# Running the experts of 24 of 32 token tiles on gathered rows, in a transformer layer on one core

## The reference, cut to what matters

```python
x1 = _layer_norm(x + attn_out, ln1_w, ln1_b)
gates = jax.nn.softmax(x1 @ gate_w.T + gate_b, axis=-1)
_, top_idx = jax.lax.top_k(gates, TOP_K)          # TOP_K = 2 of NE = 8
top_gates = jnp.take_along_axis(gates, top_idx, axis=-1)
expert_outputs = jnp.einsum('bsd,efd->bsef', x1, expert_w) + expert_b[None, None]
sel = jnp.take_along_axis(expert_outputs, top_idx[..., None], axis=2)
moe_out = jnp.sum(sel * top_gates[..., None], axis=2)
return _layer_norm(x1 + moe_out, ln2_w, ln2_b)
```

## Time and profile before

| | |
|---|---|
| median of three runs | 1448.19 us (1446.72 to 1450.09) |
| the profiled execution's own time | 1447.28 us |
| its span | 1445.5 us |
| TensorE busy | 1384.9 us, 96% |
| VectorE busy | 1089.6 us, 75% |
| ScalarE busy | 783.6 us, 54% |
| GpSimd busy | 428.0 us, 30% |
| mean granted TensorE clock | 0.993 |

### The profile page before, as it was taken

The page is one execution under the profiler, slowest core; times in us unless marked ns, Lnnn a source line. Parts: engine busy times, 40 slices in busy tenths (PEclk is TensorE's granted clock), DMA queues, the critical chain, the costliest instruction groups (busy, mean ns, idle before and its releaser), DMA issues.

```text
span 1445.5 us, 28119 instructions
## 1 busy us (share of the span) xinstructions
PE 1384.9 (96%) x9600; PEld 773.2 (53%) x9600; DVE 1089.6 (75%) x2736; ACT 783.6 (54%) x1707; POOL 428.0 (30%) x707
## 2 busy tenths in 40 slices
PE   7899999999999999999999999999999999999995
PEld 6767655554455445354656655555443355555542
DVE  3765877887787887778655897888778787888745
ACT  3235365555665555666655445554656467665651
POOL 4434522322232231122343543333121110111233
PEclk9999999999999999999999999999999999999997
DMA  3865422230211121120116232222120011111100
GB/s 116 201 172 128 124 57 61 58 85 21 63 46 46 38 62 33 40 57 20 50 49 156 79 90 68 57 57 65 29 60 21 22 24 29 33 32 33 34 23 12
DMA packets 152560, 88.57 MB, mean 61 GB/s; under 512 B 114430, under 2 KB 145974, under 8 KB 152163
## 3 DMA queue, kind: packets, MB, share of 16 engines
q1 hardware_dynamic: 152419, 86.78, 23.2%
HBM read 60.71 MB, written 25.43 MB: 60 GB/s over the span
## 4 chain that ended last, share of the span: by engine, by line
PE 44%; DVE 4%; ACT 3%; issue 2%; SPq 2%; DMA 2%; POOL 1%; POOLq 0%; DVEq 0%; ACTq 0%
PE bank L1537 11%; PE bank L1424 10%; PE bank L1401 8%; PE bank L1373 7%; ACT pbuf L978 2%; DVE mxs L1065 2%; SPq L806 1%; DMA qs<-nmT 1%; PE bank L1494 1%; PE bank L1377 1%; PE bank L1406 1%; PE bank L1513 1%; PE bank L1472 1%; PE bank L1480 1%; PE bank L1523 1%
## 5 line engine op out<-in xcount | busy, mean ns | idle before, releaser
L1065 DVE TENSOR_REDUCE mxs<-bank 128x1 f32<-128x512 f32 (+3 forms) x1120 | 709.4, 667 | 150.1 <-PE bank L1373 79.6
L978 ACT ACTIVATE pbuf<-bank 128x512 f32<-128x512 f32 (+1 forms) x1112 | 588.6, 599 | 326.1 <-PE bank L1401 151.0
L1401 PE MATMUL bank<-qs,ks 99*128 99x256 bf16 (+3 forms) x1536 | 420.7, 319 | 16.4 <-DMA qs<-nmT 10.9
L1373 PE MATMUL bank<-ks,qs 96*128 96x512 bf16 (+3 forms) x1280 | 423.0, 349 | 4.9 <-DVE mxs L1065 2.5
L1424 PE MATMUL bank<-pbuf,vcur 128*17 128x256 f32 (+3 forms) x3072 | 253.5, 469 | 0.3
L1401 PEld LDWEIGHTS bank<-qs,ks 99*128 99x128 bf16 x1536 | 142.3, 98 | 172.1 <-issue 56.3
L1537 PE MATMUL bank<-ew,x1T 128*128 128x512 f32 x464 | 222.4, 601 | 0.4 <-DVE mxs L1065 0.3
L1373 PEld LDWEIGHTS bank<-ks,qs 96*128 96x128 bf16 x1280 | 123.3, 98 | 129.7 <-issue 40.6
L1424 PEld LDWEIGHTS bank<-pbuf,vcur 128*17 128x17 f32 x3072 | 79.8, 97 | 147.4 <-issue 109.6
L1537 PEld LDWEIGHTS bank<-ew,x1T 128*128 128x128 f32 x464 | 82.0, 190 | 72.3 <-issue 60.8
L958 ACT ACTIVATE etmp<-bank,small 128x256 f32<-128x256 f32 x116 | 48.7, 471 | 80.1 <-PE bank L1537 80.1
(11 more groups left out here) (279 smaller groups left out, 1746.2 us busy)
## 6 DMA issues: line engine op xcount, KB each, us to landing
vcur<-v_scratch SPq DMA_DIRECT2D x92, 136.0 KB, 2.3
parts_scratch<-parts SPq DMA_DIRECT2D x29, 384.0 KB, 3.3
xw<-windows SPq DMA_DIRECT2D x29, 256.0 KB, 2.8
qs<-parts_scratch SPq DMA_DIRECT2D x32, 192.0 KB, 3.3
ks<-parts_scratch SPq DMA_DIRECT2D x28, 192.0 KB, 3.4
qs<-parts_scratch SPq DMA_DIRECT2D x32, 128.0 KB, 3.1
v_scratch<-vst SPq DMA_DIRECT2D x29, 136.0 KB, 2.4
x_scratch<-x SPq DMA_DIRECT2D x29, 128.0 KB, 1.7
```

Of the source, the lines that this page charges most:

```text
L978: nc.scalar.activation(pbuf[:, u0:u0 + heads, nj * P - cols:nj * P], bk[:, 0:heads * cols].rearrange("p (h t) -> p h t", h=heads), ACT.Exp)\
L1065: v.reduce_max(mxs[:, j * HJ + h:j * HJ + h + heads, c], bk[:, 0:heads * cols].rearrange("p (h t) -> p h t", h=heads), AX_X)\
L1373: last = mm(bk[:, x * cols:(x + 1) * cols].rearrange("p (n t) -> p n t", t=P), qs5[0:KR, pos % QRING, j, head, :], ks5[0:KR, kslot, 0:cols ...
L1401: last = mm(bk[:, x * cols:(x + 1) * cols].rearrange("p (n t) -> p n t", t=P), ks5[0:KR + NPART, kslot, kb % GT, head, :], qs5[0:KR + NPAR ...
```

## The change

The first 24 tiles (`SPARSE`) of the order of the `d_` and `f_` steps take another way through the experts; the last 8 stay dense. They are handled in 3 chunks of 8 tiles (`CHUNK`):

- For each tile, five small VectorE steps (`f_A`, `f_A12`, `f_as`, `f_Rb`, `f_gt`) and one on TensorE (`f_rk`, two small bf16 multiplications) count how many rows of the chunk went to the same expert before each row. `f_acc0` adds x1 and the expert bias into `rD`. `f_st` stores x1 and this sum to DRAM; the next tile's `d_res` waits for the one store and its `d_aff` for the other.
- After 8 tiles, `t_cnt` and `t_tab` (15 small VectorE instructions) work out for each of a row's two choices its place in a list of 23 blocks of 128 rows (`BLOCKS`), each block with one expert only. `t_sc` is 16 indirect transfers from GpSimd that scatter each row's number and its weight to these places in DRAM; `t_id` loads the list back in pieces of 8 bytes.
- For each of the 23 blocks: SP reads the block's expert from a register and loads its matrix, 256 KB (`s_w`), GpSimd gathers 128 rows of x1 (`s_g`), TensorE transposes them (`s_T`) and multiplies them with the one expert (`s_e`, four 128x256 instructions), ScalarE copies twice (`s_Tc`, `s_ec`, the second with the weight as scale), SP stores the block (`s_st`).
- For each tile again: `b_load` brings back the sum of `f_acc0`, `b_g1` and `b_g2` are indirect transfers from GpSimd that gather the row's two results and add them in; the `h_` steps are the `g_` steps in buffers of their own, without `g_y`.
- All this has 16 KB of its own in each partition (`gathering`). `pbuf` gives them up: `VRUN` goes from 4 to 2, so a `pv` run covers 2 key tiles and there are 192 runs in place of 100.
- `plan()` has the new steps, with 1300 ns for each indirect transfer on GpSimd and 2200 ns until it has landed (`INDIRECT`).

The core of the diff:

```diff
-VRUN = 4
+VRUN = 2
...
+INDIRECT = {"s_g": 2200, "b_g1": 2200, "b_g2": 2200, "t_sc": 2200}
...
+SPARSE = 24
+CHUNK = 8
+CHUNKS = SPARSE // CHUNK
+BLOCKS = 2 * CHUNK + NE - 1
...
+            add("f_A", T, "DVE", 100, ("f_ixf", T), ("t_tab", c - 1), ("w_tri8", 0))
+            add("f_A12", T, "DVE", 90, ("f_A", T), ("f_rk", T - 1), ("f_as", T - 1))
+            add("f_rk", T, "PE", 200, ("f_A12", T), ("f_as", T - 1), ("w_lists", 0))
+            add("f_as", T, "DVE", 90, ("f_rk", T), ("t_cnt", c - 1))
+            add("f_Rb", T, "DVE", 90, ("f_rk", T), ("t_tab", c - 1))
+            add("f_gt", T, "DVE", 90, ("f_top", T), ("t_sc", c - 1))
+            add("f_st", T, "SP", 900, ("f_acc0", T))
...
+                add("t_sc", c, "POOL", 2 * CHUNK * 1300, ("t_tab", c), ("load_dummy", 0))
+                add("t_id", c, "SP", 2500, ("t_sc", c), ("s_st", c * BLOCKS - 1))
...
+                    add("s_w", u + x, "SP", 900, ("t_tab", c), ("s_e", u + x - 2), ("w_o", 0))
+                    add("s_g", u + x, "POOL", 1300, ("t_id", c), ("f_st", last), ("s_T", u + x - 2))
+                    add("s_T", u + x, "PE", 215, ("s_g", u + x), ("s_e", u + x - 1))
+                    add("s_Tc", u + x, "ACT", 300, ("s_T", u + x), ("s_e", u + x - 2))
+                    add("s_e", u + x, "PE", 900, ("s_Tc", u + x), ("s_w", u + x))
+                    add("s_ec", u + x, "ACT", 300, ("s_e", u + x), ("s_st", u + x - 2))
+                    add("s_st", u + x, "SP", 900, ("s_ec", u + x))
...
+        gathering = sb("gathering", [P, 4096])
...
+                elif name == "t_sc":
+                    pool.wait_ge(tab_step, TABS * (T + 1))
+                    pool.wait_ge(dummy_stored, 16 * CHUNKS)
+                    for x in range(2 * CHUNK):
+                        pool.indirect_dma_start(id_dram[T], bass.IndirectOffsetOnAxis(ap=placed[:, x:x + 1], axis=0),
+                                                own[:, x // 2, x % 2, :], None).then_inc(ids_stored, 16)
...
+                    pool.indirect_dma_start(accB, None, ys_dram[T // CHUNK], bass.IndirectOffsetOnAxis(
+                        ap=placed[:, 2 * (T % CHUNK) + k:2 * (T % CHUNK) + k + 1], axis=0), compute_op=ALU.add)\
+                        .then_inc(gathered, 16)
```

More of the change, by code:

```diff
@@ L307, in stage_steps @@
-        add("f_e0", T, "PE", 1720, ("d_x1Tc", T))
+        if T < SPARSE:
+            c, u = T // CHUNK, T // CHUNK * BLOCKS
+            add("f_acc0", T, "DVE", 330, ("f_b", T), ("d_aff", T))
+            add("f_A", T, "DVE", 100, ("f_ixf", T), ("t_tab", c - 1), ("w_tri8", 0))
[5 more added lines that the diff above has]
+            add("f_st", T, "SP", 900, ("f_acc0", T))
+            i = T % CHUNK
+            last = c * CHUNK + CHUNK - 1
+            add("b_load", T, "SP", 450, ("f_st", T), ("h_aff2", T - 1))
+            add("b_g1", T, "POOL", 1300, ("t_tab", c), ("s_st", u + BLOCKS - 1), ("b_load", T))
+            add("b_g2", T, "POOL", 1300, ("b_g1", T))
+            back = c * CHUNK + CHUNK - 1 + 6 + 1.2 + (2.6 + 0.5 * i if c < CHUNKS - 1 else 1.3 + 0.25 * i)
+            rows["b_load", T] = *rows["b_load", T][:2], back - 0.3, rows["b_load", T][3]
+            rows["b_g1", T] = *rows["b_g1", T][:2], back - 0.2, rows["b_g1", T][3]
+            rows["b_g2", T] = *rows["b_g2", T][:2], back - 0.1, rows["b_g2", T][3]
+            if i == CHUNK - 1:
+                add("t_cnt", c, "PE", 150, ("f_as", T))
+                add("t_tab", c, "DVE", 3500, ("t_cnt", c), ("f_Rb", T), ("f_gt", T), ("b_g2", c * CHUNK - 1), ("s_st", c * BLOCKS - 1), ("w_tri8", 0))
+                add("t_sc", c, "POOL", 2 * CHUNK * 1300, ("t_tab", c), ("load_dummy", 0))
+                add("t_id", c, "SP", 2500, ("t_sc", c), ("s_st", c * BLOCKS - 1))
+                base = last + 6 + 1.2
+                for name in ("t_cnt", "t_tab", "t_sc", "t_id"):
+                    rows[name, c] = *rows[name, c][:2], base, rows[name, c][3]
+                for x in range(BLOCKS):
+                    add("s_w", u + x, "SP", 900, ("t_tab", c), ("s_e", u + x - 2), ("w_o", 0))
[5 more added lines that the diff above has]
+                    add("s_st", u + x, "SP", 900, ("s_ec", u + x))
+                    for k, name in enumerate(("s_w", "s_g", "s_T", "s_Tc", "s_e", "s_ec", "s_st")):
+                        rows[name, u + x] = *rows[name, u + x][:2], base + 0.1 + (2.5 if c < CHUNKS - 1 else 1.2) * x / BLOCKS + k / 100, rows[name, u + x][3]
+            add("h_load", T, "SP", 450, ("b_g2", T), ("st0", tile), ("h_store", T - 1))
+            add("h_st", T, "DVE", 330, ("b_g2", T))
+            add("h_mv", T, "DVE", 100, ("h_st", T))
+            add("h_rstd2", T, "POOL", 950, ("h_mv", T))
+            add("h_xb", T, "POOL", 700, ("h_load", T), ("h_rstd2", T))
+            add("h_norm2", T, "DVE", 370, ("h_mv", T))
+            add("h_aff2", T, "DVE", 370, ("h_norm2", T), ("h_xb", T))
+            add("h_zst", T, "DVE", 330, ("h_aff2", T))
+            add("h_zmv", T, "DVE", 100, ("h_zst", T))
+            add("h_rstd3", T, "POOL", 950, ("h_zmv", T))
+            add("h_norm3", T, "DVE", 320, ("h_rstd3", T))
+            add("h_store", T, "SP", 450, ("h_norm3", T))
+            for k, name in enumerate(("load", "st", "mv", "rstd2", "xb", "norm2", "aff2", "zst", "zmv", "rstd3", "norm3", "store")):
+                rows["h_" + name, T] = *rows["h_" + name, T][:2], back + k / 32, rows["h_" + name, T][3]
+            continue
@@ L1291, in _ @@
                 elif name in ("f_e0c", "f_e2c"):
                     k = int(name[3])
-                    half = e0_half if k == 0 else e2_half
                     dve.wait_ge(*fill(name[:4], T))
@@ L1532, in _ @@
                     mm(bk[:, 0:E], wT[f], ebp[:, :], start=True, stop=True).then_inc(filled[b], 1)
+                elif name == "f_rk":
+                    pe.wait_ge(hot12_ready, T + 1)
+                    pe.wait_ge(lists_ready, LISTS)
+                    last = mm(bk[:, 0:NE], tri, hot12, start=True, stop=T % CHUNK == 0)
+                    if T % CHUNK:
+                        pe.wait_ge(hotsum_ready, T)
+                        last = mm(bk[:, 0:NE], one, hotsum, start=False, stop=True)
+                    last.then_inc(filled[b], 1)
+                elif name == "t_cnt":
+                    pe.wait_ge(hotsum_ready, (T + 1) * CHUNK)
+                    mm(bk[:, 0:NE], one, hotsum, start=True, stop=True).then_inc(filled[b], 1)
+                elif name == "s_T":
+                    pe.wait_ge(xslot_loaded[T % 2], 16 * (T // 2 + 1))
+                    for c in range(EC):
+                        last = tr(bk[:, c * P:(c + 1) * P], xslot[T % 2][:, c * P:(c + 1) * P], idf[:, :])
+                    last.then_inc(filled[b], 1)
+                elif name == "s_e":
+                    pe.wait_ge(*drain("s_T", T))
+                    pe.wait_ge(wslot_loaded[T % 2], 16 * (T // 2 + 1))
+                    for c in range(EC):
+                        last = mm(bk[:, 0:E], xTslot[T % 2][:, c, :], wslot[T % 2][:, c, :], start=c == 0, stop=c == EC - 1)
+                    last.then_inc(filled[b], 1)
                 elif name in ("f_e0", "f_e1", "f_e2", "f_e3"):
```

397 lines of the change are left out of this document (335 added, 62 removed).

## The result

The changed kernel takes 1471.06 us (median of 5 executions, 1464.71 to 1473.57) against 1448.19; the ratio is 1.0147, with a 95% interval of 1.0123 to 1.017. The forecast was 1395 us, with 1362 to 1441 for 8 in 10. So it is slower, by about 23 us, and outside the range. The profiled execution took 1464.71 us, the fastest of the five, of which 1462.6 are the span shown here.

A forecast was written before the change was run, and what follows sets the result against it. TensorE's work was taken to bound the kernel: -78.9 us there brings the profiled 1447.3 to 1368.4, plus 16 for VectorE and 10 for late transfers gives 1394.4, with 0.9 for the median 1395 us; 8 in 10 from 1362 to 1441.

The forecast's parts named there:

- VectorE's pace: From 166 to 600 us VectorE, at 87%, would make the stretch 16 us longer than TensorE alone; bounds 0 and 51.
- late transfers and GpSimd's bursts: Late normalisations behind 16 indirect transfers in one piece and late gathers at the blocks' `s_T`: 10 us, bounds 0 and 138.
- The added work: On TensorE: 69 blocks 75.2 us, ranking 2.9 us, 92 more `pv` runs 12.9 us.
- ScalarE's longer wait for `pv`: Short `pbuf` rival: `ex` waits 92 times more, 110 us, mostly covered; if two fifths reach TensorE, 1439 us; chance 15%.
- The run length: `VRUN` from 4 to 2: 92 more `pv` runs at 0.14 us each on TensorE, 12.9 us.
- What another engine takes back: VectorE's added steps against TensorE's need, by stretch: 16 us from 166 to 600 us, nothing in the later stretches.
- Transfers and queues: About 50 MB more transfers, 216 more SP issues, 165 indirect transfers at 1.3 us on GpSimd: 10 us in all.
- SP's queue: Sign of failure: one queue, SP's above all, holds `nm_st` back for several us in each job.
- The serial path of a tile: The next tile's `d_res` waits for this tile's stored sum: 20 to 30 us, covered by a tile's 39 us, costed at nothing.

The follow-up runs named there:

- The half steps: The kernel before with half of the expert matmuls of its first 24 tiles left out: 1394.20 us in the old order, 1385.99 us when planned for.
- the kernel with neither: The changed kernel with the 48 adding gathers and the 48 scatters left out, order kept: 1432.04 us, ratio 0.9885.

## Why the prediction was wrong

The sum was -78.9 us for TensorE, +16 for VectorE's pace, +10 for late transfers and GpSimd's bursts, -53 in all. Measured is +22.9, so 76 us are missing. By its own steps:

**The added work was sized well.** The blocks cost 69 us against 75.2. The issue of a plain gather or a scatter took 0.97 to 0.99 us against 1.3, that of an adding gather 1.63. ScalarE's longer wait for `pv` came and was mostly covered. The run length cost 18.4 us against 12.9.

**"What another engine takes back": the removed work was not worth its time.** This is the first step that failed. It asked only whether VectorE's sum fits, took 16 us, and said of three of the four stretches that they need nothing. Measured on whole steps, in the changed kernel's order without transfers and blocks, 107.0 of 167.0 us came back: the term is 60 us, with the longer front and back of a tile in it. Up to about 600 us the 16 us were nearly right, as 19 were lost; the 34 us lost behind that, at 81% of VectorE, stand where the prediction had nothing. The half steps say the same with nothing else changed: of 85 us taken out, 57 came back in the old order and 63 in a new one, 67% and 74%, which for 169.9 us would be a loss of 45 to 56. What TensorE waits for in those 60 us is shown only in part (the transposed maxima, 9 us of 28 in the half steps).

**"Transfers and queues": the size was taken from the wrong place.** This is the second failure, 32 us against 44 in the first. The term was 10 us, drawn from TensorE's waits for late small transfers. It was put on the gathers of the blocks, which cost 4 us of waiting, and the adding gathers had no term. By differences these cost 17.6 + 19.4 = 37 us, and the scatters 22.9 - 17.6 = 5. With 5.5 us more for the run length and 6 less for the blocks, the four come to the missing 76 us. They have to, since they are the differences of neighbouring kernels in one row; each is good to a few us. The chain of the changed kernel, for one tile of the back stage: start us, us, what:

```profile
999.38 1.67 POOL gathering L1126
1001.05 2.32 issue
...
1003.60 4.85 DMA gathering<-ys_scratch,gathering
1008.45 0.02 issue
1008.47 0.43 DVE gathering L1644
...
1017.03 1.65 POOL gathering L1126
```

Two gathers one behind the other, 4.2 and 4.9 us each from the start of the issue to the landing, where the order was laid out for 1.3 + 2.2; then `h_st`, and 18 us from one tile to the next. The prediction did name SP's queue as what could break it. SP's standing behind these gathers was worth 2 to 4 us.

**TensorE's clock had no term.** The sum takes full speed throughout. The mean granted clock is 0.972 of 1462.6 us, where it was 0.993 of 1445.5, so up to some 30 us of full-speed time went at the lower level. They are no fifth sum beside the others but part of what the waits in them cost.

**"The serial path of a tile" was costed at nothing, and once it cost 5 us.** The wait of the chain in the second run of scatters of the changed kernel:

```profile
861.74 9.05 DMA acc_scratch<-rD
...
870.91 0.44 DVE rD L1432
```

A store that takes 2.1 us in the median took 9.05 during the scatters (in the kernel with neither, none of these stores took over 3.2), `d_res` waited for it, and TensorE stood 4.9 us until 871. It is most of what the scatters cost there (33.6 against 26.8 us).

**What stays open.** Why some programs have the long stops of TensorE's semaphores and others don't: of the twelve profiled kernels with scatters five have waits on "remote", with stops of 4.8 to 15.0 us, all in runs of scatters; no kernel without scatters has any. Two programs with the same order and the same steps up to 490 us (the changed kernel and the one without adding gathers) differ in whether one is there. Only one execution of each kernel was profiled, so whether a kernel's other executions have them is not known. Open are also the other half of the adding gathers' cost, and most of what holds TensorE back once the expert steps are gone.

## What to carry to other kernels

Work taken off a full engine is worth its time only while the rest keeps that engine fed (here 64% to 74% of it came back); take out as much with nothing added first, as one run, and read the rate from it. In an order written out by hand or by a planner, a new kind of step has to be measured before it is planned, since in an in-order queue everything behind waits for a transfer that lands later than planned: here 0.4 us later in the median and up to 1.4 in the chain shown, for 48 gathers, and 13 to 16 us of the time went once the planner had the measured costs. And a median alone can mislead when one suspect is left out: compare the same instructions in both traces, stretch by stretch.

## What was not expected of the hardware

While GpSimd issued 16 scatters of 128 rows of 8 bytes back to back (0.96 us each, every 1.26 us), other work could stand still. A plain store of 128 KB landed after 9.05 us in place of 2.1. In five programs the semaphores that TensorE's instructions raise stood still for up to 15.0 us (some 13 us behind the instruction in the case shown), while GpSimd's own issues went on at 0.95 to 0.96 us. The Trainium skill ("DMA: Bandwidth & Descriptors", section on SWDGE, HWDGE and iDMA) has VectorE lock GpSimd out of the rings of its descriptors in VectorE's two-port modes. The issues here show no such lock: 954 to 1267 ns for a scatter of the changed kernel, with VectorE busy 24 of the 34 us from 852 on. No row tells whether any of VectorE's instructions there ran in such a mode.

A gather that adds costs GpSimd 1.63 us against 0.98 for the plain one of the same 128 rows.
